# A fused attention and feed-forward block: a timetable shifted by one step, with the weighted latents scaled on GpSimd instead of VectorE

## The reference

```python
xn = layernorm(x)
h  = layernorm(xn) * ln_scale + ln_bias          # the attention's own norm
c_q, c_kv = h @ w_down_q.T, h @ w_down_kv.T       # latents, 64 wide each
q, k, v = c_q @ w_up_q.T, c_kv @ w_up_k.T, c_kv @ w_up_v.T   # 16 heads of 64
q, k = rope(q), rope(k)
attn = softmax(q @ k.T / 8)                       # 256 x 256 for each head
a = (attn @ v) @ w_out.T + xn
y = square(relu(xn @ W_fc.T)) @ W_proj.T          # 512 hidden
ffn = spikes(y, 5 steps) / 5                      # a count of thresholds that y passes
out = x + a + ffn
```

## Time and profile before

| what | value |
|---|---|
| median of 3 runs | 1368.28 us (1367.05 to 1368.46) |
| the profiled execution | 1363.53 us, of it 1361.7 us span |
| PE busy | 1133.1 us, 83% of the span |
| DVE busy | 1048.2 us, 77% |
| ACT busy | 823.7 us, 60% |
| POOL busy | 793.1 us, 58% |
| mean granted TensorE clock | 0.917 |
| DMA busy, share of 16 engines | q1 (SP's transfers) 47.3%, q10 (ACT's) 13.2% |

### The profile page before, as it was taken

How to read it: one execution, slowest core, us unless ns; L and a number is a source line. 1 busy time by engine, 2 the same in 40 slices (tenths; PEclk the granted TensorE clock), 3 DMA queues, 4 the chain that set the end, 5 groups by cost and what they waited for, 6 DMA issues and landing times.

```text
span 1361.7 us, 25592 instructions
## 1 busy us (share of the span) xinstructions
PE 1133.1 (83%) x6880; PEld 773.4 (57%) x6880; DVE 1048.2 (77%) x1478; ACT 823.7 (60%) x2881; POOL 793.1 (58%) x773
## 2 busy tenths in 40 slices
PE   4687888888888898888898888898888888888886
PEld 3455565555555565555565555565565565565553
DVE  3777787877787878788877787877788877787872
ACT  2566655666656666665666655666665666655661
POOL 3565575565575575575565575565575565575560
PEclk9888888998888999988998888998888998888998
DMA  4455656656656656756755756655656656656654
GB/s 143 113 149 150 170 148 170 167 141 163 170 143 179 162 145 171 177 144 164 177 147 154 177 139 169 174 146 157 170 147 168 173 145 159 171 140 174 171 154 93
DMA packets 88665, 213.67 MB, mean 157 GB/s; under 512 B 21952, under 2 KB 38592, under 8 KB 88512
## 3 DMA queue, kind: packets, MB, share of 16 engines
q1 hardware_dynamic: 68160, 146.25, 47.3%
q10 hardware_dynamic: 20480, 67.13, 13.2%
HBM read 7.77 MB, written 4.19 MB: 9 GB/s over the span
## 4 chain that ended last, share of the span: by engine, by line
issue 38%; PE 16%; POOL 16%; SPq 12%; DVE 9%; DMA 4%; ACT 4%; POOLq 1%; ACTq 0%; DVEq 0%
SPq L244 12%; POOL partner L725 7%; PE ps_s L292 5%; PE ps_u L308 5%; DMA gathered<-turned 4%; DVE turned L591 3%; POOL qk L728 3%; POOL relu_sb L757 2%; ACT prob L471 2%; PE ps_b L383 2%; DVE neg_max L582 1%; PE ps_a L344 1%; POOL rstd L740 1%; DVE qk L577 1%; POOL resid L750 1%
## 5 line engine op out<-in xcount | busy, mean ns | idle before, releaser
L471 ACT ACTIVATE prob<-ps_s,neg_max 128x256 f32<-128x256 f32 x1024 | 472.1, 474 | 392.7 <-DVE neg_max L582 358.7
L725 POOL TENSOR_TENSOR partner<-partner,rope_sb 128x512 f32<-128x512 f32 x256 | 326.5, 1275 | 493.5 <-DMA partner<-raw 492.7
L582 DVE TENSOR_REDUCE neg_max<-ps_s 128x4 f32<-128x1024 f32 x256 | 312.7, 1222 | 201.1 <-PE ps_s L292 197.8
L728 POOL TENSOR_TENSOR qk<-qk,partner 128x512 f32<-128x512 f32 x256 | 327.7, 1280 | 20.1
L308 PE MATMUL ps_u<-gathered,ckv 128*64 128x256 f32 x2048 | 307.4, 425 | 35.2 <-DMA gathered<-turned 31.8
L292 PE MATMUL ps_s<-qk 64*128 64x256 f32 x2048 | 319.1, 434 | 7.0 <-POOL qk L728 7.0
L591 DVE STREAM_TRANSPOSE turned<-prob 128x1024 f32<-128x1024 f32 x256 | 315.9, 1234 | 0.1
L292 PEld LDWEIGHTS ps_s<-qk 64*128 64x128 f32 x2048 | 191.6, 202 | 131.3 <-issue 85.1
L577 DVE TENSOR_TENSOR qk<-ps_qk,rope_sb 128x512 f32<-128x512 f32 x256 | 171.3, 669 | 61.3 <-PE ps_qk L283 60.1
L471 ACT ACTIVATION_READ_ACCUMULATOR prob<-ps_s,neg_max 128x1 f32 x1024 | 208.9, 204 | 0.0
L308 PEld LDWEIGHTS ps_u<-gathered,ckv 128*64 128x64 f32 x2048 | 135.4, 147 | 127.4 <-issue 48.9
(11 more groups left out here) (57 smaller groups left out, 961.3 us busy)
## 6 DMA issues: line engine op xcount, KB each, us to landing
gathered<-turned SPq DMA_DIRECT2D x1024, 128.0 KB, 2.4
partner<-raw ACTq DMA_DIRECT2D x256, 256.0 KB, 2.4
x_sb<-in_x SPq DMA_DIRECT2D x32, 128.0 KB, 2.5
out<-out_sb SPq DMA_DIRECT2D x32, 128.0 KB, 2.7
turned<-in_wup SPq DMA_DIRECT2D x2, 512.0 KB, 5.9
rope_sb<-in_rope SPq DMA_DIRECT2D x1, 512.0 KB, 7.0
turned<-in_wo_t SPq DMA_DIRECT2D x1, 512.0 KB, 8.4
turned<-in_sel SPq DMA_DIRECT2D x1, 512.0 KB, 9.1
```

Of the source, the lines that this page charges most:

```text
L471: last = nc.scalar.activation(prob[:, s % 2, :, h, :, t, :].rearrange("p j k c -> p k j c"), ps_s[:, s % 2, h, t, :].rearrange("p (k j c) ...
L582: nc.vector.tensor_reduce(neg_max[:, s % 2, :, :], ps_s[:, s % 2, :, :, :], AXIS_X, ALU.max, negate=True).then_inc(max_ready, 1)
L725: nc.gpsimd.tensor_tensor(other, other, sin_sb, ALU.mult).then_inc(sin_ready, 1)
L728: nc.gpsimd.tensor_tensor(qk[:, s % 4, :, :], qk[:, s % 4, :, :], other, ALU.add).then_inc(rope_done, 1)
```

## The change

The leads of all stages but the last grow by one step. The extras get new places, and some of them new engines:

- `normalise_u` goes from DVE to POOL, at p=7,0,1,2. POOL reads it from SBUF: ACT makes a copy of each spread chunk (`copy_broadcast`, right behind the exponentials of p=7,0,1,2), double-buffered in `scale_sb`.
- The split of the inverse sums goes from DVE to POOL (`split_sums`, p=2), the high part of the latents from DVE to ACT (`lead_latents`, p=3).
- `normalise` moves from p=2 to p=1, the transposes to p=2, `copy_inputs` to p=2, `latents` to p=3, `latents_by_token` to p=1, `ffn_in` to p=7,0, the squares to p=0,1, `ffn_out` to p=4,5, `integrate` to p=5,6, `transpose_rden` and `copy_rden` to p=6 (the copy now behind the exponentials), `broadcast_rden` to p=7,0,1,2, `attention_out` to p=3 to 6, `add_spikes`, `transpose_sum` and `finish` to p=7.
- `transpose_sum` writes ps_u, so `weigh_latents` of p=7 waits for `finish`, and that of p=6 for `copy_rden`.
- SP issues the 16 DMAs of a move in one go (at p=0 and 4). The residual is added in place by POOL (p=3) and copied by one more DMA a batch on SP (`keep_residual`).

```diff
-LEAD = {"project": 11, "rope": 9, "scores": 7, "turn": 6, "multiply": 0}
+LEAD = {"project": 12, "rope": 10, "scores": 8, "turn": 7, "multiply": 0}
...
@@ SP
-            def move(g, s, half):
+            def move(g, s):
                 par = (s // GROUP) % 2
-                if half == 0:
-                    sp.wait_ge(turn_done, done(g))
-                    sp.sem_inc(sp_waited, 1)
-                    sp.wait_ge(u_ready, done(g - 2 * GROUP))
-                for rows in (2 * half, 2 * half + 1):
+                sp.wait_ge(turn_done, done(g))
+                sp.sem_inc(sp_waited, 1)
+                sp.wait_ge(u_ready, done(g - 2 * GROUP))
+                for rows in range(Q):
...
+            def keep_residual(par):
+                sp.dma_start(resid[:, par, :], xn_sb[:, par, :, :].rearrange("p t d -> p (t d)"))\
+                    .then_inc(copied[par], 16)
...
+                if p == 0:
+                    if not outside(b, B):
+                        sp.wait_ge(res_ready, done(b))
+                    if not outside(b, B) and not outside(b + 2, B):
+                        load_x(b + 2, b0)
+                    if not outside(b - 2, B):
+                        store(b - 2, b0)
+                    if not outside(b, B):
+                        keep_residual(b0)
                 if (s + turn) % GROUP == GROUP - 1 and not outside(g + turn, STEPS):
-                    move(g + turn, s + turn, 0)
...
+                    move(g + turn, s + turn)
@@ PE, weigh_latents
-                if s % PAIRS == 4:
+                if s % PAIRS == 6:
                     pe.wait_ge(rt_evac, done(i * UNROLL + s // PAIRS))
+                elif s % PAIRS == 7 and not outside(i * UNROLL + s // PAIRS - 1, B):
+                    pe.wait_ge(final_done, done(i * UNROLL + s // PAIRS - 1))
@@ PE, extras
+                if not outside(b - 1, B):
+                    if p < 3:
+                        broadcast_rden(b - 1, p + 1)
+                    elif p < 7:
+                        attention_out(b - 1, p - 3)
+                if p == 7:
+                    if not outside(b, B):
+                        broadcast_rden(b, 0)
+                    if not outside(b - 1, B):
+                        transpose_sum(b - 1)
+                    if not outside(b + 1, B):
+                        ffn_in(b + 1, 0, 1 - b0)
+                if not outside(b, B):
                     if p == 0:
...
+                        ffn_in(b, 1, b0)
+                    elif p in (4, 5):
+                        ffn_out(b, p - 4)
                     elif p == 6:
-                        ffn_out(n, 1)
+                        transpose_rden(b)
+                if p == 1 and not outside(b + 1, B):
+                    latents_by_token(b + 1)
                 if not outside(b + 2, B):
-                    if p == 3:
+                    if p == 2:
                         transpose_inputs(b + 2, b0)
-                    elif p == 4:
+                    elif p == 3:
                         latents(b + 2)
@@ ACT
+            def copy_broadcast(b, c):
+                act.wait_ge(bc_ready, done(CHUNKS * b + c))
+                act.wait_ge(u_norm, done(CHUNKS * b + c - 2))
+                nc.scalar.copy(scale_sb[:, c % 2, :, :], ps_b[:, :].rearrange("p (j s) -> p j s", j=2)).then_inc(bc_evac, 1)
...
+                if p < 3 and not outside(b - 1, B):
+                    copy_broadcast(b - 1, p + 1)
+                elif p == 7 and not outside(b, B):
+                    copy_broadcast(b, 0)
+                if not outside(b, B):
                     if p == 0:
...
+                        relu(b, 1)
+                    elif p == 6:
+                        copy_rden(b)
+                if not outside(b + 1, B):
+                    if p == 1:
+                        copy_latents(b + 1, 1 - b0)
+                    elif p == 7:
+                        relu(b + 1, 0)
                 if not outside(b + 2, B):
-                    if p == 2:
...
+                    if p == 1:
+                        normalise(b + 2, b0, 0, i + 1)
+                        normalise(b + 2, b0, 1, i + 1)
+                    elif p == 2:
+                        copy_inputs(b + 2, b0)
                     elif p == 3:
-                        copy_inputs(b + 2)
+                        lead_latents(b + 2, b0)
@@ POOL
+            def normalise_u(b, c):
+                pool.wait_ge(bc_evac, done(CHUNKS * b + c))
+                pool.wait_ge(u_evac, done(PAIRS * b + 2 * c + 1))
+                if not outside(b - 1, B):
+                    pool.wait_ge(out_part, done(CHUNKS * (b - 1) + c))
+                nc.gpsimd.tensor_tensor(u_n[:, 2 * c:2 * c + 2, :], u_raw[:, 2 * c:2 * c + 2, :],
+                                        scale_sb[:, c % 2, :, :], ALU.mult).then_inc(u_norm, 1)
...
                     inverse_std(b + 2)
                 if not outside(g + LEAD["rope"], STEPS):
                     add_rotated(g + LEAD["rope"], s + LEAD["rope"], i)
-                if p in (2, 3) and not outside(b + 1, B):
-                    square(b + 1, p - 2)
-                if p == 6 and not outside(b + 1, B):
-                    residual(b + 1, 1 - b0)
+                if p < 3 and not outside(b - 1, B):
+                    normalise_u(b - 1, p + 1)
+                elif p == 7 and not outside(b, B):
+                    normalise_u(b, 0)
+                if p < 2 and not outside(b, B):
+                    square(b, p)
+                if p == 2 and not outside(b, B):
+                    split_sums(b)
+                if p == 3 and not outside(b + 2, B):
+                    residual(b + 2, b0)
```

More of the change, by code:

```diff
@@ L162, in build @@
         moved = [sem(f"moved{i}") for i in range(2)]
+        copied = [sem(f"copied{i}") for i in range(2)]
         u_ready = sem("u_ready")
@@ L257, in step @@
                 b, turn = i * UNROLL + b0, LEAD["turn"]
-                if p == 0 and not outside(b, B) and not outside(b + 2, B):
-                    sp.wait_ge(res_ready, done(b))
-                    load_x(b + 2, b0)
-                if (s + turn) % GROUP == GROUP - 1 and not outside(g + turn, STEPS):
-                    move(g + turn, s + turn, 0)
[L263 to L266, removed]
+                if p == 0:
[7 more added lines that the diff above has]
+                        keep_residual(b0)
+                if (s + turn) % GROUP == GROUP - 1 and not outside(g + turn, STEPS):
+                    move(g + turn, s + turn)
             run(sp, prologue, step)
+            store(B - 1, (B - 1) % 2)
             for par in range(2):
@@ L447, in step @@
                     scores(g + LEAD["scores"], s + LEAD["scores"])
-                if p == 4 and not outside(b, B):
-                    transpose_rden(b)
                 extras(b, b0, p)
@@ L452, in step @@
                     project(g + LEAD["project"], s + LEAD["project"], i)
-                if p == 5 and not outside(b + 1, B):
-                    ffn_out(b + 1, 0)
                 if not outside(g, STEPS):
@@ L499, in copy_u, with normalise @@
                 nc.scalar.copy(u_raw[:, pair, :], ps_u[:, 0, :]).then_inc(u_evac, 1)
-            def normalise(n, par, which):
+            def normalise(n, par, which, i):
                 act.wait_ge(shift_ready, done(n))
                 if which == 0:
-                    act.wait_ge(res_ready, done(n - 2))
-                    act.wait_ge(tr_ready, done(n - 2))
+                    if not outside(n - 2, B):
+                        act.wait_ge(copied[par], 16 * i)
                     dst, ready = xn_sb[:, par, :, :], xn_ready
@@ L518, in copy_inputs, with lead_latents @@
                 nc.scalar.activation(h_t[:, :], ps_a[:, 0:S], ACT.Identity, bias=ln_sb[:, 1:2], scale=ln_sb[:, 0:1])
-                nc.scalar.copy(xn_t[:, :], ps_a[:, S:2 * S]).then_inc(tr_evac, 1)
+                nc.scalar.copy(xn_t[:, par, :], ps_a[:, S:2 * S]).then_inc(tr_evac, 1)
+            def lead_latents(n, par):
+                act.wait_ge(cc_ready, done(n))
+                for which in range(2):
+                    rows = slice(which * L, (which + 1) * L)
+                    last = nc.scalar.copy(latent[rows, par, which, :], ps_a[rows, 0:S])
+                last.then_inc(latent_hi, 1)
             def copy_latents(n, par):
@@ L539, in prologue @@
                 for which in range(2):
-                    normalise(0, 0, which)
-                copy_inputs(0)
+                    normalise(0, 0, which, 0)
+                copy_inputs(0, 0)
+                lead_latents(0, 0)
             def step(i, s):
@@ L627, in split_latents @@
             def split_latents(n, par):
-                dve.wait_ge(cc_ready, done(n))
-                for which in range(2):
-                    rows = slice(which * L, (which + 1) * L)
-                    last = nc.vector.tensor_copy(latent[rows, par, which, :], ps_a[rows, 0:S])
-                last.then_inc(latent_hi, 1)
```

(3 more changed lines are left out.)

142 lines of the change are left out of this document (58 added, 84 removed).

## The result

The changed kernel takes **1393.87 us** (median of 4 executions, 1389.03 to 1395.34) against 1368.37 for the kernel before on the same chip: ratio 1.0182, 95% interval 1.0156 to 1.0209. It is slower by 25.5 us; the forecast was slower by 9.7. The profiled execution took 1395.34 us, of it 1393.5 span.

What follows compares the result with a forecast made beforehand. Order of work bound the kernel, 40.75 us a batch. The new chain's 39.5 plus 1.3 and 0.2 for clock falls gave 41.0; +8 over 31.9 batches and +2 on 1363.5 gave 1373.5, plus 4.8 to the median: 1378 us, range 1322 to 1410.

Steps and rivals of the forecast that it cites:

- Steps 1 to 3: From p=0's scores: POOL's rope at 3.8 us, inverse deviation by 10.8, ACT's norms waiting 2.1, exponentials of p=2 at 14.3.
- the rival of dear small instructions: POOL's two sum-splitting instructions take 1.275 us each, p=5's rope comes 1.85 later: 42.4 us a batch, 1423; chance 0.04.
- Steps 4 to 6: p=2 to p=5: ACT done with p=2 at 18.0 us, scores of p=5 at 24.5, p=5's work ending at 28.8.
- The signs that I named for single steps: Maxima to maxima: about 7.4 us at p=1 to 2, 5.8 at p=6, 5 at p=7, under 4.4 at p=0 and p=5.
- Steps 7 and 8: p=6 takes 5.8 us, weigh waiting for ACT's copy behind the exponentials; p=7 takes 5.0, ending the batch at 39.5.
- The clock: PE's stop at p=2 lowers the clock, 1.3 us a batch; a second fall costs 1.8 in one batch of eight, 0.2.
- second fall every batch: PE's stops at p=6 and p=7 drop the clock every batch: 42.6 us a batch, 1429; chance 0.12.
- faster: Same chain, clock unharmed or costs absorbed, restart at p=2 under 1.1 us: 39.5 to 40.5 a batch, 1330 to 1362; chance 0.35.
- Much faster: The norms are not late, so their 2.1 us wait and the clock's fall go: 37.4 us a batch, 1263; chance 0.06.
- the part on what is added: Added work raises ACT to 32.8 us a batch and POOL to 30.6, all well under 40.75, so no queue bounds.
- 255/8 batches x 0.25: The whole run: 31.9 batches, each 0.25 us longer (41.0 against 40.75), add 8 us.
- The tail: The last batch's spreading follows the last matmuls, three chunks through copy and POOL: +2 us; the longer lead adds no more.

Runs made afterwards that it cites:

- experiment 5: The changed kernel with POOL's inverse deviation moved from p=1 to p=0, behind the rope: 1358.91 us.
- experiment 7: The changed kernel with both ACT's already implied waits left out and the inverse deviation moved to p=0: 1330.04 us.
- experiment 1: The changed kernel without ACT waits that others already imply, 27 instructions a loop body fewer: 1370.04 us.
- experiment 8: experiment 1 with ACT's copy of the inverse sums (copy_rden) at p=6 put ahead of the exponentials: 1317.92 us.
- experiment 3: The changed kernel with 96 idle semaphore increments on ACT ahead of the loop: 1370.45 us.
- experiment 10: The changed kernel with multiplications back on DVE, inverse deviation at p=0, copy_rden ahead of the exponentials and finish ahead of turn at p=7: 1268.42 us.
- experiment 12: experiment 1 with inverse deviation at p=0, copy_rden ahead of the exponentials and finish ahead of turn, multiplications left on POOL: 1265.68 us.
- experiment 4: experiment 1 with 70 idle semaphore increments on ACT ahead of the loop: 1383.88 us.
- experiment 2: The kernel before with 30 idle semaphore increments in ACT's loop body, at p=5, 6 and 7: 1369.75 us.
- experiment 9: experiment 1 with six unused matmuls on PE at p=2, where it waits for the norms: 1342.79 us.

## Why the prediction was wrong in size

**Steps 1 to 3 (the rope, POOL's order, the late norms): right to 0.2 us,** as the timeline shows, but for PE's stop, 3.42 against 3.8. Splitting the sums on POOL takes 0.21 and 0.25 us, where I had guessed 0.35 each, so the rival of dear small instructions is out. Experiments 5 and 7 confirm the place: moving five small instructions ahead takes ACT's wait away.

**Steps 4 to 6 (p=3 to p=5): right with the clock's price.** The scores of p=5 stand at 25.91 (24.5 + 1.3 predicted), those of p=6 at 30.38 (28.8 + 1.3). The signs that I named for single steps fit less well: I had 7.4 us from the maxima of p=1 to those of p=2, and in experiment 1 these are 3.7, and 9.5 from there to p=3; the step at p=5 takes 4.47, not under 4.4.

**Steps 7 and 8: right.** 5.79 and 5.03 us measured, 5.8 and 5.0 predicted. Experiment 8 shows the cause of the first.

**The clock: right at p=2** (1.25 against 1.3), and near it at p=6. I had a second fall in one batch of eight; the changed kernel has one in 7 of 30, experiment 1 in 1 of 30. Such a fall, windows of the changed kernel around a stop of 1.90 us at p=6:

```profile
639.50:643.70 4.20, 2.31 (x17) 1.73 (x15) 3.81 (x6) 2.61 (x10) 0.00 (x0) 0.99 0.94 264
643.70:648.50 4.80, 4.80 (x25) 3.03 (x21) 1.90 (x4) 0.44 (x2) 3.83 (x4) 0.65 0.72 161
```

The step takes 7.4 us in place of 5.8, a price of 1.6 against my 1.8 (in three of the seven batches 6.5 to 6.6, and 0.8). The rival "second fall every batch" is out. The rival "faster" needed a price under 1.1. "Much faster" would have had 1263 us with the norms in time; with them in time, experiment 7 took 1330, as the rope at p=3 came next.

**What failed: the part on what is added.** I costed ACT's new instructions as ACT's time, 2.6 us a batch with much room, and closed with "no queue is the bound by its sum". I never counted them as code. ACT's body, where it lies, stops at the branch each of the 13 times that it is taken: 13 x 3.55 = 46 us of stop, of which 23.8 arrive in the time. My sum had this term at nothing. A batch with the stop takes 42.3 us against 40.9 in experiment 1: of the 3.55 us 1.4 arrive, which is about what is left when the 2.07 us that ACT would have waited for the shift are taken off. Over 13 passes that is 18 us; the clock accounts for the rest, with second falls in seven batches in place of one, less six batches of 40.2. No rival held this mechanism.

**The sum, without that term.** Experiments 1 and 3 stand for the kernel that I had predicted: 1370.04 and 1370.45 against 1378, 2 to 3 us over the kernel before beside them, where my sum had 9.7. The batch was right, but "255/8 batches x 0.25" set a steady batch (41.0) against an average with the fill (40.75; steady it is 40.79). With the longer lead 15 steps belong to fill and drain, and in experiment 1 they take 72.1 us, where 15 steady steps would take 76.8: its maxima grow by 2.0 us, not by 8. (A slip that changes nothing: 1330 less 0.3 us for each of 31.9 batches is 1320, not 1322.)

**The tail: +2 was +9.0.** Tail of the changed kernel, behind its last maxima at 1351.5:

```profile
1371.70 1.91 PE L370 MATMUL ps_a<-relu_sb,wproj_sb 128*128 128x256 f32 x4
...
1376.20 0.37 ACT L555 CAST rden_t<-ps_u 128x256 fp32r<-128x256 f32 x1 [0.90 <-PE ps_u L379]
...
1381.74 3.74 POOL L781 TENSOR_TENSOR u_n<-u_raw,scale_sb 128x512 f32<-128x512 f32 x3 [1.54 <-ACT scale_sb L560]
...
1384.19 5.41 PE L398 MATMUL ps_b<-u_n,wvo_sb 128*128 128x256 f32 x16 [0.68 <-ACT scale_sb L560]
```

I had moved three chunks behind the last matmuls. The feed-forward part, the transposition of the sums and `finish` of the batch before came there too, one after another, and the 16 matmuls at the end take 5.41 us where before they took 3.72.

**Still open.** Executions of one kernel scatter by 12 us (1362.8 to 1374.7 in experiment 1; the granted clock was 0.925 in the one and 0.912 in the other). By profiled executions experiment 1 is 11.2 us slower than before, by medians 2.05; the 9 us of the tail can't be found in the medians, and I did not separate what makes up for them.

**The chances.** Slower by over 0.2% had 0.52, and 1393.87 lies within 1322 to 1410. But that is luck: it lies there by a cause that I did not name, and with the chain that I did name the kernel equals the one before.

## What to carry to other kernels

Count the instructions that a change adds to a loop body and ahead of it, waits and increments too, for each engine; if the profile shows an engine idle by "issue" right behind the loop's branch and more packets on the instruction queue, try a shorter body, or one at another place, before anything else. Where small instructions feed a long chain, their place in the queue counts more than their engine: one line moved (experiment 8) was worth 52 us, and changing the engine (experiments 10 and 12) nothing in sum once the order was right. A gain measured in one timetable may be taken back by the next wait, so repairs are to be tried together.

## What the hardware showed that I had not expected

- From a taken branch of the loop to ACT's next instruction 3.54 to 3.59 us pass in the changed kernel and 0.23 to 0.28 in the kernels without the stop, by where the body lies; five packets of 8 KB per pass go with it.
- 13 stops of this kind cost 23.4 us in the changed kernel (against experiment 3), 13.8 in the same timetable with 27 instructions fewer in ACT's body (experiment 4 against 1), and nothing that the medians show in the old timetable (experiment 2).
- PE's stop of 1.90 us at p=6 lets the clock fall in some batches and not in others: 7, 1 and 8 of 30 in the changed kernel and in experiments 1 and 9.
